# Another order for the prologue and the first row of an adaLN attention/FFN block

## The chip, the cores and the metric

The kernel runs on one core of one Trainium2 chip. The metric is device time in microseconds of one launch; before the change it is 679.94 us (median of 3 runs, 679.27 to 681.49).

## The reference, cut to what matters

```python
mod = (silu(c) @ wmod).reshape(B, 6, 1, D)         # B = 8, D = 256
sa, ca, ga, sb, cb, gb = mod[:, 0..5]              # ga, gb: magnitude at least 0.25
h = layernorm(x) * (1 + ca) + sa                   # x: 8 x 2048 x 256
q, k, v = split(h @ w_qkv + b_qkv)                 # 8 heads of 64
scores = einsum('bhld,bhle->bhde', q, k) / 8       # 64 x 64 per head: over the sequence
attn = softmax(scores)
o = (v @ attn) @ w_fc + b_fc + h
x = x + ga * (layernorm(o) * gamma + beta)
h = layernorm(x) * (1 + cb) + sb
xr, xk = mu * h + (1 - mu) * previous_token(h)     # mu_r, mu_k
x = x + gb * sigmoid(xr @ W_r.T) * (relu(xk @ W_k.T)**2 @ W_v.T)
```

## The kernel before, in words

The scores of a head are 64 x 64 and sum over the sequence. So the kernel first forms, per batch row, the 256 x 256 Gram matrix of the normalised x ("gram"), multiplies it from both sides with the scaled q and k weights (`gram_q`, `scores`), takes the softmax, folds v weights, attention and output weights into one 256 x 256 matrix M (`wv_attn`, the v product, and `make_m`), and then applies M to each chunk (`attention`). All is fp32; the products with M and with W_v are made of three products of high and low parts, `m_hi`, `m_lo`, `z_hi`, `z_lo` (helper `mm3`, L1239 to L1241).

A batch row (b = 0..7) has four chunks j of 512 tokens, and each chunk four tiles of 128 tokens. The rows are software-pipelined: `row_steps(b)` does the second half of row b (attention, residual and second layernorm, FFN) beside the first half of row b + 1 (statistics, normalisation, Gram matrix, softmax, M). The prologue is the first half of row 0, and `row_steps(0, first=True)` has an order of its own; rows 1 to 6 are a hardware loop, and row 7 has `last_row`.

The order on each engine is written out by hand, and engines wait for each other on semaphores with counts. An engine works through its own program in order. Its parts, by engine:

- VectorE (DVE): `stats_a` (L902), `make_z` (L912, the first normalisation), `low_z` (L992), softmax (L1070 to L1087), `take_vb` (L863), `make_m` (L1094 `m_sb`, L1097 `m_hi`, L1099 `m_lo`), `prep_now` (L1039, waits for the row `ca` from DRAM), `make_x2` (L924 and L929), `stats_2` (L935 to L945), `mix_r` and `mix_k` (L957, L966), `prep_qk` (L1047), `low_k` (L1000).
- GpSimd (POOL): `rstd_a` (L460 to L472: nine small operations, the reciprocal root of a chunk's variance), `rstd_o` (L485, L487), `rstd_2` (L478, L480), `bias_wv` (L509, which completes `wv_aug`), `fill_x2` (L492, a DMA from its queue that adds x to the rows waiting in `x2`).
- ScalarE (ACT): `copy_z_hi` (L618), `squares` (L652), `copy_pv` (L642), `copy_weights` (L612), `prep_base_qk` (L709, L710), `make_z2` (L717), `copy_h2` (L661), `scale_r`, `scale_k` (L670, L679), `take_r`, `take_k`.
- TensorE (PE): `turn_and_gram` (transposes L1348, Gram products L1355), `attention` (L1239 to L1241 into `att`), `turn_z2` (L1392), `ffn_r` (L1408), `ffn_k` (L1425), `ffn_out` (L1239 to L1241 into `work`), `turn_ffn` (L1330, transposes of the three FFN weights), `wv_attn` (L1479), `make_m` (L1488), `bias_v` (L1292), `mod_b_columns` (L1263).
- SyncE (SP): loads and stores. `next_ca(1)` loads the row `ca` of row 1 (L312) once M of row 0 is ready.

There are eight PSUM banks: `gram`, `tr0` and `tr1` (all transposes), `att0` and `att1` (attention's output), `work0` to `work2` (FFN). `attention(b, j)` may write `att` only when VectorE has read the chunk before it out of there (`t_done`). `turn_and_gram(b, j)` for j of 2 and 3 waits until ScalarE has taken the transposed `z2` of chunk j - 2 out of `tr` (`h2_ready`).

The first part of TensorE's row 0 was

```python
attention(b, 0)
turn_and_gram(n, 0)
attention(b, 1)
turn_and_gram(n, 1)
turn_z2(b, 0)
attention(b, 2)
turn_and_gram(n, 2)
```

with n = b + 1.

## Time and profile before

| | us |
|---|---|
| median of 3 runs | 679.94 |
| lowest and highest | 679.27, 681.49 |
| the profiled execution, its own time | 681.61 |
| its span, first to last instruction | 679.8 |
| PE busy | 654.6 |
| DVE busy | 567.8 |
| ACT busy | 457.0 |
| POOL busy | 294.0 |

The profile is of one execution. Times in it count from the first instruction. Prologue and row 0 up to the last step that the change moves lie in the first 98 us. The granted TensorE clock is 0.991 on average over the span: 1.00 means 2.4 GHz, 0.50 means 1.2 GHz. Busy times of matmuls are modelled ends, so starts are the safer numbers.

### The profile page before, as it was taken

How to read it: one execution, taken by the hardware profiler on the slowest of the kernel's cores; microseconds unless marked ns; L12 is line 12 of the kernel's file. 1: busy time of each engine (PE TensorE's matmuls, PEld its weight loads, DVE VectorE, ACT ScalarE, POOL GpSimd, SP SyncE). 2: the span in 40 equal slices, each digit the busy share in tenths (PEclk: the TensorE clock that was granted, in tenths of full speed). 3: DMA queues.
4: the chain of work that ended last, by engine and by line, in shares of the span. 5: the costliest groups of instructions: out<-in, count | busy, mean ns of one | idle time of the engine just before them, and what ended most of it. 6: DMA issues, size and time to landing. Idle time of an engine off the chain costs nothing.

```text
span 679.8 us, 12488 instructions
## 1 busy us (share of the span) xinstructions
PE 654.6 (96%) x3968; PEld 535.5 (79%) x3968; DVE 567.8 (84%) x1328; ACT 457.0 (67%) x983; POOL 294.0 (43%) x499
## 2 busy tenths in 40 slices
PE   8978799999999999999999999999999999999896
PEld 6657777889869887889878888798878888697665
DVE  5893988889798897889888897889888897859973
ACT  1423767676966779667867769577776769667662
POOL 5263452764318442574227542383327643215230
PEclk9988999999999999999999999999999999999999
DMA  8859237384854958086765758268673737537325
GB/s 315 224 166 198 89 113 160 61 182 123 195 111 83 230 109 208 31 167 165 162 123 100 170 125 204 79 108 224 129 156 62 128 84 169 101 76 154 63 32 92
DMA packets 90985, 93.04 MB, mean 137 GB/s; under 512 B 4224, under 2 KB 89000, under 8 KB 90960
## 3 DMA queue, kind: packets, MB, share of 16 engines
q0 software_dynamic: 33264, 33.03, 32.9%
q1 hardware_dynamic: 55344, 55.97, 26.1%
q10 hardware_dynamic: 2352, 3.73, 1.5%
q8 instruction: 12, 0.20, 0.1%
...
HBM read 42.84 MB, written 33.10 MB: 112 GB/s over the span
## 4 chain that ended last, share of the span: by engine, by line
PE 85%; DVE 7%; POOL 2%; ACT 2%; DMA 2%; issue 2%; DVEq 0%; POOLq 0%; ACTq 0%
PE work L1408 14%; PE work L1425 14%; PE gram L1355 10%; PE att L1239 4%; PE work L1239 4%; PE gram L1488 4%; PE work L1240 4%; PE work L1241 4%; PE att L1241 4%; PE att L1240 4%; PE tr L1392 4%; PE att L1460 4%; PE tr L1348 3%; PE att L1479 2%; PE gram L1470 1%
## 5 line engine op out<-in xcount | busy, mean ns | idle before, releaser
L478 POOL TENSOR_TENSOR rs<-ve,neg_half 128x4 f32<-128x4 f32 x32 | 37.4, 1170 | 179.3 <-DVE ve L945 179.3
L1425 PE MATMUL work<-mx,w_k_t 128*128 128x512 f32 x244 | 109.9, 592 | 0.0
L1408 PE MATMUL work<-w_r_t,mx 128*128 128x256 f32 x464 | 106.0, 381 | 0.3 <-DVE mx L983 0.3
L717 ACT ACTIVATE z<-x,nm,rs 128x256 f32<-128x256 f32 x128 | 66.4, 594 | 46.5 <-POOL nm L480 46.5
L1408 PEld LDWEIGHTS work<-w_r_t,mx 128*128 128x128 f32 x464 | 85.8, 190 | 11.8 <-DVE mx L983 0.5
L1355 PE MATMUL gram<-z 128*128 128x256 f32 (+1 forms) x512 | 89.1, 327 | 0.0
L1355 PEld LDWEIGHTS gram<-z 128*128 128x128 f32 x512 | 79.8, 191 | 6.6
L1425 PEld LDWEIGHTS work<-mx,w_k_t 128*128 128x128 f32 x244 | 46.3, 190 | 46.0 <-issue 42.4
L1239 PE MATMUL att<-m_lo,z_hi 128*128 128x256 f32 x248 | 74.9, 302 | 3.8 <-issue 2.0
L1239 PE MATMUL work<-wvf_lo,k_hi 128*128 128x256 f32 x248 | 72.0, 290 | 2.5 <-issue 2.5
L1240 PE MATMUL att<-m_hi,z_hi 128*128 128x256 f32 x248 | 70.8, 285 | 0.0
L1241 PE MATMUL att<-m_hi,z_lo 128*128 128x256 f32 x248 | 70.7, 285 | 0.0
L1241 PE MATMUL work<-wvf_hi,k_lo 128*128 128x256 f32 x248 | 69.1, 279 | 0.0
L1240 PE MATMUL work<-wvf_hi,k_hi 128*128 128x256 f32 x248 | 69.1, 278 | 0.0
L652 ACT ACTIVATE sq<-att 128x256 f32<-128x256 f32 x124 | 45.7, 381 | 33.1 <-PE att L1241 33.1
L924 DVE SCALAR_TENSOR_TENSOR t_buf<-att,rs_o,g_row 128x256 f32<-128x256 f32 x124 | 51.4, 477 | 10.7 <-POOL rs_o L487 9.9
L485 POOL TENSOR_TENSOR ve_o<-ssq,eps_att 128x4 f32<-128x4 f32 x32 | 17.0, 531 | 94.0 <-ACT sq L652 94.0
L661 ACT ACTIVATE h2t<-tr,mod_now 128x512 f32<-128x512 f32 x64 | 46.4, 781 | 15.2 <-PE tr L1392 15.2
L1000 DVE TENSOR_TENSOR k_lo<-work,k_hi 128x512 fp32r<-128x512 f32 x60 | 40.6, 689 | 18.7 <-ACT k_hi L702 18.5
L492 POOL DMA_DIRECT2D x<-in_L_attn_x_dram x32 | 55.2, 1823 | 0.0
L957 DVE SCALAR_TENSOR_TENSOR mx<-h2t,rest_col,mx 128x512 f32<-128x512 f32 x56 | 39.4, 745 | 17.5 <-ACT mx L670 17.5
L1239 PEld LDWEIGHTS att<-m_lo,z_hi 128*128 128x128 f32 x248 | 48.0, 193 | 7.5 <-issue 7.5
...
## 6 DMA issues: line engine op xcount, KB each, us to landing
...
```

The source lines that it names most:

```text
L492: nc.gpsimd.dma_start(x2[:, j], x_v[b, j], accum_op=ALU.add).then_inc(x2_filled[j], 16)
L652: ins = nc.scalar.activation(sq[:, t], att_banks(j, alone)[t // 2][:, (t % 2) * D:(t % 2 + 1) * D], ACT.Square, scale=float(D) ** -0.5, ac ...
L661: nc.scalar.activation(h2t[:, h, 1 + j * CT:1 + (j + 1) * CT], tr[h][:], ACT.Identity, bias=mod_now[:, h:h + 1], scale=mod_now[:, 2 + h:3 ...
L717: ins = nc.scalar.activation(z2[:, t], x2[:, j, t], ACT.Identity, bias=nm_2[:, s, t:t + 1], scale=rs_2[:, s, t:t + 1])
L924: ins = nc.vector.scalar_tensor_tensor(t_buf[:, t], att_banks(j, alone)[t // 2][:, (t % 2) * D:(t % 2 + 1) * D], rs_o[:, s, t:t + 1], g_ro ...
L1000: nc.vector.tensor_tensor(lo[:, h], k_banks(alone)[h][:], hi[:, h].bitcast(F32), ALU.subtract).then_inc(k_lo_ready, 1)
L1239: mm(dst, s_hi, m_lo, start=start, stop=False)
L1240: mm(dst, s_hi, m_hi, start=False, stop=False)
L1241: return mm(dst, s_lo, m_hi, start=False, stop=stop)
L1355: ins = mm(gram[:, k * D:(k + 1) * D - k * P], z[:, j % 2, t, k * P:(k + 1) * P], z[:, j % 2, t, k * P:D], start=(j == 0 and t == 0 and k ...
L1408: ins = mm(r_banks(alone)[q][:, (t % 2) * D:(t % 2 + 1) * D], mixed(j)[0][:, ch, tile], w_r_t[:, ch], start=(ch == 0), stop=(ch == KD - 1))
L1425: ins = mm(k_banks(alone)[dh][:], w_k_t[:, ch, rows_dh], mixed(j)[1][:, ch], start=(ch == 0), stop=(ch == KD - 1))
```

## The change

VectorE, prologue: the softmax of row 0 and `take_vb` come before the statistics of row 1; the statistics of chunks 2 and 3 of row 1 move from row 0 into the prologue, before `make_m(0)`; `make_z(1, 1)` goes behind `make_m(0)`. In row 0, `make_z(1, 2)` moves from behind `stats_2(0, 1)` to before `low_z(1, 0)`.

GpSimd: `bias_wv` comes before both `rstd_a` of the prologue; the four `fill_x2` are issued in two pairs between the `rstd_a` calls; `rstd_a(1, 2)` moves into the prologue; `rstd_o(0, 1)` goes before `rstd_2(0, 0)`.

TensorE: `wv_attn(0)` goes before `turn_ffn`. In row 0, chunk 0 of row 1 is transposed and multiplied before the first attention; `attention(0, 1)` writes the banks `work0` and `work1`, which the FFN doesn't use yet, and follows `attention(0, 0)` at once; `attention(0, 2)` goes before `turn_z2(0, 0)`. `turn_and_gram(b, 0)` waits on `m_step` (the Gram bank is read) in place of `m_ready` (M is split).

ScalarE: `copy_pv(0)` before the copies of the FFN weights; `squares(0, 1)` read the spare banks.

```diff
@@ -77,8 +77,9 @@
         def k_banks(alone):
             return (gram, work[2]) if alone else (work[1], work[2])
 
-        def att_banks(j, alone):
-
+        def att_banks(j, alone, spare=False):
+            if spare:
+                return work[0:2]
             return tr if alone and j == 1 else att
 
 
@@ -518,17 +519,16 @@
 
                 n = b + 1
                 rstd_o(b, 0)
-                if not first:
+                if first:
+                    rstd_o(b, 1)
+                else:
                     add_y(b - 1, 2)
                     fill_x2(b, 2)
                 rstd_2(b, 0)
                 if first:
-
-                    rstd_o(b, 1)
-                    rstd_a(n, 2)
+                    rstd_a(n, 3)
                     rstd_2(b, 1)
                     rstd_o(b, 2)
-                    rstd_a(n, 3)
                 else:
                     rstd_o(b, 1)
                     rstd_2(b, 1)
@@ -570,11 +570,14 @@
             for j in range(CH):
                 rstd_a(0, j)
             prep_wv()
+            bias_wv()
             rstd_a(1, 0)
+            fill_x2(0, 0)
+            fill_x2(0, 1)
             rstd_a(1, 1)
-            bias_wv()
-            for j in range(CH):
-                fill_x2(0, j)
+            rstd_a(1, 2)
+            fill_x2(0, 2)
+            fill_x2(0, 3)
             row_steps(0, True, True)
             with pool.Fori(1, B - 2) as b:
                 row_steps(b, False, True)
@@ -642,14 +645,14 @@
                     nc.scalar.activation(pv_t[:, 2 * g:2 * g + 2].rearrange("p n d -> p (n d)"), att[g][:],
                                          ACT.Copy).then_inc(pv_ready, 1)
 
-            def squares(b, j, alone=False):
+            def squares(b, j, alone=False, spare=False):
 
                 i, s = CH * b + j, j % 2
                 wait_past(act, ssq_ready, i)
                 for t in range(NT):
                     if t % 2 == 0:
                         act.wait_ge(att_done, 2 * i + t // 2 + 1)
-                    ins = nc.scalar.activation(sq[:, t], att_banks(j, alone)[t // 2][:, (t % 2) * D:(t % 2 + 1) * D], ACT.Square,
+                    ins = nc.scalar.activation(sq[:, t], att_banks(j, alone, spare)[t // 2][:, (t % 2) * D:(t % 2 + 1) * D], ACT.Square,
                                                scale=float(D) ** -0.5, accum_out=ssq[:, s, t:t + 1])
                 ins.then_inc(ssq_ready, 1)
 
@@ -725,7 +728,7 @@
                 copy_z_hi(n, 0)
                 prep_base_qk(n)
                 if first:
-                    squares(b, 1)
+                    squares(b, 1, spare=True)
                     copy_z_hi(n, 1)
                     make_z2(b, 0)
                 else:
@@ -807,8 +810,8 @@
             copy_gram_low(0)
             copy_gq(0)
             exps(0)
+            copy_pv(0)
             copy_weights(2, [(w_r_t[:], tr[0]), (w_k_t[:], tr[1]), (w_v_t[:], work[0])])
-            copy_pv(0)
             row_steps(0, True)
             with act.Fori(1, B - 1) as b:
                 row_steps(b, False)
@@ -913,7 +916,7 @@
                                                   ag_a[:, j, 7, t:t + 1], ALU.subtract, ALU.mult)
                 ins.then_inc(z_ready, 1)
 
-            def make_x2(b, j, mixes=0, alone=False):
+            def make_x2(b, j, mixes=0, alone=False, spare=False):
 
                 i, s = CH * b + j, j % 2
                 wait_past(dve, x2_ready, i)
@@ -921,8 +924,8 @@
                     dve.wait_ge(xk_mixed, CH * b + mixes)
                 dve.wait_ge(rs_o_ready, i + 1)
                 for t in range(NT):
-                    ins = nc.vector.scalar_tensor_tensor(t_buf[:, t], att_banks(j, alone)[t // 2][:, (t % 2) * D:(t % 2 + 1) * D],
-                                                         rs_o[:, s, t:t + 1], g_row[:], ALU.mult, ALU.mult)
+                    src = att_banks(j, alone, spare)[t // 2][:, (t % 2) * D:(t % 2 + 1) * D]
+                    ins = nc.vector.scalar_tensor_tensor(t_buf[:, t], src, rs_o[:, s, t:t + 1], g_row[:], ALU.mult, ALU.mult)
                 ins.then_inc(t_done, 1)
                 dve.wait_ge(t_done, i + 1)
                 dve.wait_ge(x2_filled[j], 16 * (b + 1))
@@ -1103,16 +1106,15 @@
                 n = b + 1
                 take_g(b)
                 prep_now(n)
+                if first:
+                    make_z(n, 2)
                 low_z(n, 0)
                 make_x2(b, 0)
                 stats_2(b, 0)
                 if first:
-                    stats_a(n, 2)
-                    stats_a(n, 3)
                     low_z(n, 1)
-                    make_x2(b, 1)
+                    make_x2(b, 1, spare=True)
                     stats_2(b, 1)
-                    make_z(n, 2)
                 else:
                     low_k(b - 1, 3)
                     make_z(n, 2)
@@ -1210,15 +1212,17 @@
             low_z(0, 3)
             centre_fc()
             make_rest()
-            stats_a(1, 0)
-            stats_a(1, 1)
             softmax_dif(0)
             take_vb()
             softmax_norm(0)
+            stats_a(1, 0)
+            stats_a(1, 1)
+            take_mod_col(1, mod_b_done, work[2])
+            stats_a(1, 2)
             make_z(1, 0)
+            stats_a(1, 3)
+            make_m(0)
             make_z(1, 1)
-            take_mod_col(1, mod_b_done, work[2])
-            make_m(0)
             dve.wait_ge(mod_col_ready, 2)
             dve.wait_ge(rest_ready, 1)
             dve.wait_ge(w_copied, 5)
@@ -1348,7 +1352,7 @@
                         ins = nc.tensor.transpose(tr[h][:, t * P:(t + 1) * P], z[:, j % 2, t, h * P:(h + 1) * P], ident[:])
                     ins.then_inc(z_turned, 1)
                 if j == 0 and not first:
-                    pe.wait_ge(m_ready, b)
+                    pe.wait_ge(m_step, 2 * b - 1)
                 for t in range(NT):
                     for k in range(KD):
 
@@ -1357,11 +1361,15 @@
                                  skip_group_check=True)
                 ins.then_inc(z_used, 1)
 
-            def attention(b, j, alone=False):
+            def attention(b, j, alone=False, spare=False, after_spare=False):
                 i = CH * b + j
                 pe.wait_ge(m_ready, b + 1)
                 pe.wait_ge(z_lo_ready, 2 * i + 2)
-                if not alone:
+                if after_spare:
+                    pe.wait_ge(t_done, i - 1)
+                elif spare:
+                    pass
+                elif not alone:
                     wait_past(pe, t_done, i)
                 elif j == 1:
                     pe.wait_ge(h2_ready, 2 * CH * b)
@@ -1371,7 +1379,7 @@
                     for t in (2 * q, 2 * q + 1):
                         tile = slice(t * P, (t + 1) * P)
                         for k in range(KD):
-                            ins = mm3(att_banks(j, alone)[q][:, (t % 2) * D:(t % 2 + 1) * D],
+                            ins = mm3(att_banks(j, alone, spare)[q][:, (t % 2) * D:(t % 2 + 1) * D],
                                       (z_hi[:, j, k, tile], z_lo[:, j, k, tile], m_hi[:, k], m_lo[:, k]),
                                       start=(k == 0), stop=(k == KD - 1))
                     ins.then_inc(att_done, 1)
@@ -1491,17 +1499,23 @@
             def row_steps(b, first):
 
                 n = b + 1
-                attention(b, 0)
-                turn_and_gram(n, 0)
-                if not first:
+                if first:
+                    turn_and_gram(n, 0)
+                    attention(b, 0)
+                    attention(b, 1, spare=True)
+                    turn_and_gram(n, 1)
+                    attention(b, 2, after_spare=True)
+                    turn_z2(b, 0)
+                else:
+                    attention(b, 0)
+                    turn_and_gram(n, 0)
                     ffn_r(b - 1, 3)
                     ffn_k(b - 1, 3)
-                attention(b, 1)
-                if not first:
+                    attention(b, 1)
                     ffn_out(b - 1, 3)
-                turn_and_gram(n, 1)
-                turn_z2(b, 0)
-                attention(b, 2)
+                    turn_and_gram(n, 1)
+                    turn_z2(b, 0)
+                    attention(b, 2)
                 turn_and_gram(n, 2)
                 ffn_r(b, 0)
                 ffn_k(b, 0)
@@ -1563,8 +1577,8 @@
             scores(0)
             bias_v()
             mod_b_columns()
+            wv_attn(0)
             turn_ffn()
-            wv_attn(0)
             pe.wait_ge(fc_ready, 1)
             make_m(0)
             pe.wait_ge(w_copied, 5)
```

TensorE from the scores to the first attention, before (`y` holds the FFN weights that are transposed, `gq` and `wfc_c` are the operands of `make_m`):

```order
L1470 MATMUL gram<-wqk_aug,gq 64x64 x16
L1292 MATMUL work<-mod_col,wqkv_sb 128x8 x8
L1263 MATMUL work<-silu,h2t 128x8 x8
L1330 MATMUL tr<-ident,y 128x128 x8
L1330 MATMUL work<-ident,y 128x128 x4
L1479 MATMUL att<-wv_aug,attn 128x256 x4
L1488 MATMUL gram<-wfc_c,gq 128x256 x8
L1239 MATMUL att<-m_lo,z_hi 128x256
L1240 MATMUL att<-m_hi,z_hi 128x256
```

and in the changed kernel:

```order
L1478 MATMUL gram<-wqk_aug,gq 64x64 x16
L1296 MATMUL work<-mod_col,wqkv_sb 128x8 x8
L1267 MATMUL work<-silu,h2t 128x8 x8
L1487 MATMUL att<-wv_aug,attn 128x256 x4
L1334 MATMUL tr<-ident,y 128x128 x8
L1334 MATMUL work<-ident,y 128x128 x4
L1496 MATMUL gram<-wfc_c,gq 128x256 x8
L1352 MATMUL tr<-ident,z 128x128 x8
L1359 MATMUL gram<-z 128x256
```

The v product (`att<-wv_aug,attn`) now stands before the 12 transposes, and the transposes and Gram products of chunk 0 of row 1 (`tr<-ident,z`) before attention.

VectorE from the start of M's last steps to the normalisation of chunk 2, before:

```order
L1094 TENSOR_TENSOR m_sb<-gram,res 128x512
L1097 CAST m_hi<-m_sb 128x512
L1099 TENSOR_TENSOR m_lo<-m_sb,m_hi 128x512
L1018 COPY g_row<-rows 128x256
L1019 COPY mod_now<-mod_col 128x4
L1039 TENSOR_SCALAR neg_d<-rows 128x1
L1040 COPY d_now<-mod_col 128x2
L992 TENSOR_TENSOR z_lo<-tr,z_hi 128x512 x2
L924 SCALAR_TENSOR_TENSOR t_buf<-att,rs_o,g_row 128x256 x4
L929 TENSOR_TENSOR x<-t_buf,x 128x1024
L935 BN_STATS st<-x 128x6 x4
```

and in the changed kernel:

```order
L1102 TENSOR_TENSOR m_lo<-m_sb,m_hi 128x512
L915 TENSOR_SCALAR z<-x_in,ag_a 128x255 x4
L1021 COPY g_row<-rows 128x256
L1022 COPY mod_now<-mod_col 128x4
L1042 TENSOR_SCALAR neg_d<-rows 128x1
L1043 COPY d_now<-mod_col 128x2
L915 TENSOR_SCALAR z<-x_in,ag_a 128x255 x4
L995 TENSOR_TENSOR z_lo<-tr,z_hi 128x512 x2
L928 SCALAR_TENSOR_TENSOR t_buf<-att,rs_o,g_row 128x256 x4
L932 TENSOR_TENSOR x<-t_buf,x 128x1024
L938 BN_STATS st<-x 128x6 x4
```

Two normalisations (`z<-x_in`) have come into this stretch: that of chunk 1 behind `m_lo`, and that of chunk 2 behind the wait for `rows` (the row `ca`).

## Rows read from the trace of the kernel before

**Rows 1.** TensorE's waits, 40 to 150 us, then 93 to 680: total, times, longest.

```profile
PE att L1479 <- POOL wv_aug L509: 2.2, 1, 2.2
PE att L1239 <- issue: 2.0, 1, 2.0
PE tr L1348 <- DVE z L912: 1.5, 1, 1.5
...
PE work L1239 <- issue: 2.5, 3, 0.9
```

**Rows 2.** Timeline, 41 to 48 us: start, us, engine, line, out<-in, count, [idle before].

```profile
41.00 1.15 PE L1470 MATMUL gram<-wqk_aug,gq 128*64 128x64 f32 x32 [0.69 <-ACT gq L633]
43.89 1.93 PE L1263 MATMUL work<-silu,h2t 128*128 128x8 f32 x16
44.76 0.86 DVE L1070 TENSOR_REDUCE s_max<-gram 64x4 f32<-64x256 f32 x2
46.54 0.63 DVE L863 TENSOR_SCALAR vb_col<-work,bv_col 128x8 f32<-128x8 f32 x4
47.08 0.41 DVE L1081 TENSOR_REDUCE s_sum<-s_exp 128x4 f32<-128x256 f32 x1
```

**Rows 3.** Timeline, 45 to 60 us.

```profile
45.68 1.13 PE L1330 MATMUL tr<-ident,y 128*128 128x128 f32 x8
48.65 3.69 DVE L912 TENSOR_SCALAR z<-x_in,ag_a 128x255 f32<-128x255 f32 x8
49.71 5.47 POOL L492 DMA_DIRECT2D x<-in_L_attn_x_dram  x4
49.90 3.69 PE L1479 MATMUL att<-wv_aug,attn 128*128 128x256 f32 x8 [2.24 <-POOL wv_aug L509]
54.36 3.69 PE L1488 MATMUL gram<-wfc_c,gq 128*128 128x256 f32 x16 [0.78 <-ACT gq L642]
59.28 0.69 DVE L1099 TENSOR_TENSOR m_lo<-m_sb,m_hi 128x512 fp32r<-128x512 f32 x1
```

**Rows 4.** Windows: stretch, its length, busy of each engine, granted clock, DMA.

```profile
46.60:46.80 0.20, 0.20 (x3) 0.20 (x2) 0.20 (x2) 0.20 (x1) 0.20 (x3) 0.50 1.03 343
53.40:53.60 0.20, 0.18 (x1) 0.00 (x0) 0.00 (x0) 0.00 (x0) 0.20 (x2) 1.00 1.08 174
60.20:60.40 0.20, 0.20 (x2) 0.20 (x3) 0.06 (x1) 0.00 (x0) 0.00 (x0) 0.54 1.15 184
```

**Rows 5.** Windows: PE, PEld, DVE, ACT, POOL busy, granted clock, DMA.

```profile
67.30:97.70 30.40, 26.02 (x167) 22.22 (x165) 29.88 (x79) 21.09 (x48) 16.79 (x28) 1.00 0.32 104
100.00:134.00 34.00, 34.00 (x197) 26.07 (x196) 28.60 (x64) 26.13 (x54) 13.93 (x29) 1.00 0.49 112
```

**Rows 6.** Timeline of row 0, 64 to 98 us.

```profile
64.29 0.15 DVE L1039 TENSOR_SCALAR neg_d<-rows 128x1 f32<-128x1 f32 x1 [4.04 <-DMA rows<-row_scratch]
72.30 2.70 DVE L902 BATCH_NORM_STATS2 st_a<-x_in 128x6 f32<-128x256 f32 x8
78.22 1.34 ACT L670 ACTIVATE mx<-h2t,mu_col 128x512 f32<-128x512 f32 x2
81.12 1.37 DVE L912 TENSOR_SCALAR z<-x_in,ag_a 128x255 f32<-128x255 f32 x4
96.39 1.28 DVE L1000 TENSOR_TENSOR k_lo<-work,k_hi 128x512 fp32r<-128x512 f32 x2
```

**Rows 7.** GpSimd's timeline: the ends of one `rstd_a` and of another.

```profile
43.61 0.20 POOL L460 TENSOR_TENSOR ag_a<-st_a 128x4 f32<-128x4 f32 x1 [2.40 <-DVE st_a L902]
45.45 1.01 POOL L472 TENSOR_TENSOR ag_a<-ag_a,neg_half 128x4 f32<-128x4 f32 x1
...
86.41 1.19 POOL L460 TENSOR_TENSOR ag_a<-st_a 128x4 f32<-128x4 f32 x1
91.75 1.01 POOL L472 TENSOR_TENSOR ag_a<-ag_a,neg_half 128x4 f32<-128x4 f32 x1
```

**Rows 8.** The page, costliest groups: busy, mean ns of one, idle before.

```profile
L652 ACT ACTIVATE sq<-att 128x256 f32<-128x256 f32 x124 | 45.7, 381 | 33.1 <-PE att L1241 33.1
```

## The prediction, made before the changed kernel was run

> **What bounds the kernel now.** I read the page first. TensorE is busy 654.6 of 679.8 us, 96% of the span, so time can only come out of places where it stands still or runs at the lower of its two clocks. The waits of TensorE say where these are: all waits of over a microsecond lie before 93 us, and from 93 us to the end there are 5.3 us in total, of which the line with the most is 2.5 us in three places [rows 1]. Everything the change moves lies in the prologue and in row 0, before 94 us. From 100 to 134 us TensorE is busy for all 34.00 of 34.00 us [rows 5]: what arrives earlier at 97.7 us therefore arrives earlier at the end, as long as the other engines are earlier by as much.
>
> Then the timeline, where three chains follow each other.
>
> Up to 46 us it is the softmax of row 0. The scores end at 42.15 (41.00 + 1.15), but VectorE starts on the row maxima only at 44.76, behind two chunks of statistics of row 1 [rows 2]. On GpSimd the copy that completes `wv_aug` stands behind the two `rstd_a` calls which those statistics feed, and that copy is what TensorE waits for, 2.2 us, until the v product starts at 49.90 [rows 1, 3].
>
> From 49.9 to 60 us it is the v product, `make_m` on TensorE, then three VectorE steps that end at 59.97 (59.28 + 0.69) [rows 3]. TensorE waits 2.0 us for them [rows 1]. The granted clock falls twice: at about 46.6 us, behind 3.7 us of products of only 8 columns, to come back at 53.4; and at 60.2, behind the wait of 2.0 us [rows 4]. So the eight instructions of the v product take 3.69 us.
>
> From 67.30 to 97.67 us (96.39 + 1.28) it is VectorE alone: busy 29.88 of 30.40 us there [rows 5, 6]. Its program runs from `make_x2(0, 0)` to the end of `low_k(0, 0)`, and `ffn_out(0, 0)` of TensorE waits for that.
>
> **The change, part by part**, on the profiled execution (span 679.8 us, own time 681.61; the median of the three runs, 679.94, is 1.7 lower, and I take the difference over to it).
>
> *Softmax first.* VectorE starts the maxima at 42.2. Maxima, differences and the exponential took from 44.76 to 47.0, when the sums start, so they end at 44.5. `take_vb` (0.63 us) waits for `bias_v` on TensorE, which ends as the next product starts, 43.89 [rows 2]; it is through at 44.7. The sums and the division took 47.08 to 48.65, 1.57 us [rows 2, 3]: 46.3. GpSimd completes `wv_aug` at 45.1, since `bias_wv` is now ahead of both `rstd_a`. TensorE is free at 45.8 and starts the v product at 46.4 instead of 49.90.
>
> *ffn transposes behind it.* They no longer stand before the v product, and on ScalarE `copy_pv` goes ahead of their copies, so `pv_t` is made while TensorE transposes. But the clock falls at about 46.6 [rows 4], as what runs before that is not changed. I therefore keep 3.6 us for the v product: 50.0. The lower bound would be the 1.89 us that it would take with the clock up, half of 3.69, rounded up. The 12 transposes follow at the upper clock: eight are busy for 1.13 us, modelled end included [rows 3], so 1.4 to 1.7 for all: 51.4. `make_m` takes 3.69 (16 instructions against the 8 of the v product in the same time, so its row is at the upper clock): 55.1 instead of 58.05. VectorE needs its 1.9 us from there (58.05 to 59.97): `m_ready` at 57.0, **3.0 us earlier**. The statistics of chunks 0 to 3 of row 1 (four at 1.35, half of the 2.70 for two [rows 6]) and `make_z(1, 0)` lie on VectorE between 46.3 and 54, inside TensorE's 8.7 us; they cost nothing, and if that cover were gone would cost up to 1 us.
>
> *Gram of chunk 0 ahead of attention.* With the wait on `m_step` TensorE needs only the first of the three VectorE steps for `gram`, and the transposes need none. The chunk takes 3.5 us at the upper clock (82.55 to 86.0 in the timeline), so it ends at 58.6, and `attention(0, 0)` and, in the spare banks, `attention(0, 1)` follow to 61.5 and 64.4, at 2.9 each (69.1 to 72.0 in the timeline). So the wait of 2.0 and the second fall of the clock go here.
>
> *What VectorE does until `make_x2(0, 0)`.* The row `ca` is loaded only once `m_ready` is there; before, VectorE waited 4.04 us for it, to 64.29, which is 4.3 us after `m_ready` [rows 3, 6]. With the same 4.3 it comes at 61.3, plus 0.25 for the two small ones. Now `make_z(1, 2)` stands there: 1.37 us alone [rows 6], but eight such took 3.69 beside GpSimd's DMAs [rows 3], 0.46 each, so 1.37 to 1.85. Then `low_z(1, 0)`, 1.3: 64.2 to 64.7. ScalarE's squares of chunk 0 end 0.9 behind attention, 62.4, `z_hi` at 63.5, in time. I take **64.5** against 67.30: 2.8 us.
>
> *GpSimd's queue.* In its program: `rstd_a(1, 0)`, two DMAs, `rstd_a(1, 1)`, `rstd_a(1, 2)`, two DMAs, and only then `rstd_o(0, 0)`. An `rstd_a` undisturbed takes 2.85 us (43.61 to 46.46), four DMAs took 5.47 [rows 3, 7]. From 47.7 on: 3 x 2.85 + 5.5 = 14.0, so 61.8, before the squares at 62.4; `rs_o` at 63.7 is in time. `make_z(1, 1)` needs `rs_a` at 56.3 and has it. The upper bound is an `rstd_a` as at 86.41 to 92.76, 6.35 us, beside VectorE's weight preparation [rows 7]. I take 2.85, since VectorE runs mostly statistics here, as it did at 43.6.
> On that row the Trainium skill, "SBUF — State Buffer", section Who interferes with whom, says that a VectorE instruction with two SBUF inputs holds off a GpSimd instruction that reads SBUF. By it only `m_lo` here would collide, and the sum would stay; it is the ground of the third rival.
>
> *VectorE's long stretch.* Two chunks of statistics (2.70 us) and `make_z(1, 2)` (1.37) leave it [rows 6]: **4.1 us**. What shortens it uncovers waits. T is the start of `make_x2(0, 0)`. Before, `scale_r` ended at 79.56, T + 12.3, by way of the statistics, GpSimd, `make_z2`, the transposes and `copy_h2`. VectorE came to `make_z` at 81.12, T + 13.8; without the 2.70 it is there, and now at `mix_r`, at T + 11.1 [rows 6]: a wait of 1.2, of which I take 1.1, as T + 12.3 is the end of both halves. `low_z(1, 2)` then needs `z_hi` behind ScalarE's `scale_k` (1.3, as `scale_r`), four squares (1.5 [rows 8]) and the copy itself, an estimated 0.6 for the first half, as a square takes 0.38 with half the columns: T + 15.7, against VectorE free at T + 15.0: 0.6 more. Third, TensorE has done `attention(0, 2)` at 71.0 and waits for `z2` until 73.3, 2.3 us. At 2.0 us the clock had fallen [rows 1, 4], at 1.5 us (the wait for z) it had not, so I count on a fall: the eight transposes take 0.9 more, 0.6 of it passes to `copy_h2`. Sum of the waits 2.3.
> After that TensorE has `turn_and_gram(1, 2)`, `ffn_r`, `ffn_k`, two of them at 3.5 us, and reaches `attention(0, 3)` near 88, about when VectorE has freed the banks; `low_k(0, 0)` comes last, as before.
>
> *In the loop* nothing changes: there `attention` waits for a later point than the new wait on `m_step`.
>
> **Sum:** 2.8 + 4.1 − 2.3 = **4.6 us**. 679.94 − 4.6 = **675.3 us**.
>
> **The rivals.**
>
> *More is won* (0.13). The clock holds through the v product and does not fall at 73 either. `m_ready` would be 1.8 earlier, at 55.2, but then GpSimd's queue (61.8 + 1.3) sets T to 63.1. 4.2 + 4.1 − 1.7 = 6.6: 673.3. Against it: the clock row at 46.60 stands before anything that differs.
>
> *The `ca` row lands late* (0.10). It is issued at 57.0, 4 to 6 us behind the first two fills of `x2`, where it used to follow the four at a distance of 5 to 10. If it took 7.0 us instead of 4.3, VectorE would stand from 58.7 to 64, and the gain would be 4.6 − 2.7 = 1.9: 678.0. For it: transfers overlap more. Against: only two fills are in flight, not four. It is also the case in which the order does what it says and little is seen.
>
> *GpSimd comes late* (0.04), the one on the other side. `rstd_o(0, 0)` now stands behind two `rstd_a` and all four fills. If both `rstd_a` took 6.35 us [rows 7] and the fills twice their 5.47, GpSimd would be there at 61.8 + 7.0 + 5.5 = 74.3, T at 75.6, and the sum 67.3 − 75.6 + 4.1 − 1.7 = −5.9: 685.8. It decides from T = 69.7 on (67.3 + 4.1 − 1.7), that is, from GpSimd being 6.6 us later than I compute (68.4 + 1.3 = 69.7). Against it: those 6.35 us lay beside VectorE's instructions with two SBUF inputs, and hardly any stand here.
>
> **How the numbers follow.** The forecast has 0.73; its own bounds (0.5 at `make_z`, 0.6 for the clock, 0.5 at the waits) give 674.0 to 676.8. The range takes in the first rival and the second: 672.8 to 678.2. A difference under 0.3%, 2.0 us, can hardly be told from none here. Faster by more than that: the forecast, the first rival and the nearer half of a late `ca` row, 0.88; within it 0.08; slower 0.04.
>
> **What would show it.** In the profile of the changed kernel: v product from about 46.4 with some 3.6 us, `make_m` to 55, `m_lo` to 57; no wait between `make_m` and the transposes; VectorE waiting for `rows` until 61 and `make_x2(0, 0)` at 64.5; TensorE waiting some 2.3 us for `z2` and about 1 us for `h2t` behind it; `low_k(0, 0)` ending near 93 and no new idle after 100. The prediction is wrong if `rs_o` is what `make_x2(0, 0)` waits for, if the v product takes 1.9 us, or if TensorE finds a wait after 97 us that it did not have.

## The result and the profile after

| | before | after |
|---|---|---|
| median, six runs each, us | 679.61 | 676.57 |
| lowest and highest | 678.53, 681.49 | 675.36, 677.16 |
| the profiled execution, its own time | 681.61 | 675.36 |
| its span | 679.8 | 673.7 |

The ratio is 0.995, 95% interval 0.9935 to 0.9965: 3.0 us less, or 0.4%. A second comparison, on another occasion, gave 677.44 against 680.17, ratio 0.9958 (0.9945 to 0.9971), 2.7 us. The two traces above differ by more, 6.1 us. That difference is taken up below.

The page of the changed kernel, its span and the busy time of the engines:

```profile
span 673.7 us, 12495 instructions
PE 655.3 (97%) x3968; PEld 537.0 (80%) x3968; DVE 568.9 (84%) x1328; ACT 456.6 (68%) x983; POOL 289.5 (43%) x499
```

TensorE, VectorE and ScalarE work as long as before, to 1.1 us, and GpSimd 4.5 us less (289.5 against 294.0), but it is busy for less than half of the span. The span around TensorE's work is shorter. Its waits from 40 to 150 us, in the view of rows 1 (who waited for whom: total, times, longest):

```profile
PE tr L1400 <- ACT z L720: 2.2, 1, 2.2
PE tr L1352 <- ACT h2t L664: 1.2, 1, 1.2
```

The waits for `wv_aug` (2.2), for M (2.0) and for `z` of chunk 2 (1.5) of rows 1 are gone. A wait of 2.2 us for `z2` and one of 1.2 us for `h2t` have come. The timeline of the changed kernel, prologue and row 0, answers to rows 2, 3 and 6 (start, duration, engine, line, out<-in, count, idle before; SPq and POOL DMA rows are issues):

```profile
41.90 0.87 DVE L1073 TENSOR_REDUCE s_max<-gram 64x4 f32<-64x256 f32 x2
...
45.88 3.59 PE L1487 MATMUL att<-wv_aug,attn 128*128 128x256 f32 x8 [0.36 <-DVE attn L1090]
49.26 1.18 PE L1334 MATMUL tr<-ident,y 128*128 128x128 f32 x8
50.13 2.85 POOL L493 DMA_DIRECT2D x<-in_L_attn_x_dram  x2
50.71 3.62 PE L1496 MATMUL gram<-wfc_c,gq 128*128 128x256 f32 x16
...
55.55 0.69 DVE L1102 TENSOR_TENSOR m_lo<-m_sb,m_hi 128x512 fp32r<-128x512 f32 x1
56.27 0.33 SPq L313 DMA_DIRECT2D rows<-row_scratch  x1
59.45 0.15 DVE L1042 TENSOR_SCALAR neg_d<-rows 128x1 f32<-128x1 f32 x1 [1.62 <-DMA rows<-row_scratch]
59.67 2.64 POOL L493 DMA_DIRECT2D x<-in_L_attn_x_dram  x2
59.76 2.17 DVE L915 TENSOR_SCALAR z<-x_in,ag_a 128x255 f32<-128x255 f32 x4
62.26 1.29 DVE L995 TENSOR_TENSOR z_lo<-tr,z_hi 128x512 fp32r<-128x512 f32 x2 [0.33 <-ACT z_hi L621]
62.62 1.03 POOL L488 TENSOR_TENSOR rs_o<-ve_o,neg_half 128x4 f32<-128x4 f32 x1
63.68 1.66 DVE L928 SCALAR_TENSOR_TENSOR t_buf<-att,rs_o,g_row 128x256 f32<-128x256 f32 x4
...
75.86 1.42 DVE L960 SCALAR_TENSOR_TENSOR mx<-h2t,rest_col,mx 128x512 f32<-128x512 f32 x2 [0.86 <-ACT mx L673]
79.01 1.29 DVE L995 TENSOR_TENSOR z_lo<-tr,z_hi 128x512 fp32r<-128x512 f32 x2 [0.41 <-ACT z_hi L621]
90.32 1.28 DVE L1003 TENSOR_TENSOR k_lo<-work,k_hi 128x512 fp32r<-128x512 f32 x2
```

M is ready at 56.24 (55.55 + 0.69) against 59.97. `make_x2(0, 0)`, the row `t_buf<-att`, starts at 63.68 against 67.30. `low_k(0, 0)`, the last row, ends at 91.60 against 97.67. This is 6.07 us earlier, and the span is 6.1 us shorter. So nothing was won or lost behind 98 us. The same holds in all twelve other traces of this study: the span is 581.5 to 582.3 us longer than the time at which `low_k(0, 0)` ends. So the span of every traced execution below can be read from that one row. A trace shows one execution, though, and its own time can lie 2.5 us from the median of its kernel, so that it is given with each.

The granted clock of the changed kernel, windows as in rows 4:

```profile
46.00:46.20 0.20, 0.20 (x1) 0.18 (x2) 0.20 (x2) 0.00 (x0) 0.00 (x0) 0.79 1.06 348
49.20:49.40 0.20, 0.20 (x2) 0.14 (x1) 0.20 (x2) 0.00 (x0) 0.20 (x1) 0.50 0.03 10
49.60:49.80 0.20, 0.20 (x4) 0.20 (x3) 0.20 (x2) 0.20 (x1) 0.20 (x1) 1.00 0.00 0
73.40:73.60 0.20, 0.01 (x1) 0.00 (x0) 0.20 (x2) 0.20 (x1) 0.20 (x1) 0.56 0.00 0
80.00:81.00 1.00, 1.00 (x7) 0.95 (x7) 1.00 (x2) 0.00 (x0) 0.00 (x0) 0.88 0.00 1
```

The granted clock is the last number but two of a row. It falls to its lower level (1.2 GHz) at about 46.1, in the first of the eight v products, and is back (2.4 GHz) at 49.6, so that most of the ffn transposes run at the upper level. It falls once more at 73.4, in the wait for `h2t`, and is back between 80 and 81. The fall of rows 4 at 60.2 is gone.

### The profile page after: what moved, and what is told of

It reads as the page before. It is cut to its first block, busy times and chain, and to the rows that moved or that the text cites. A ratio compares the mean times of both kernels' runs of the same rounds, so it can differ in the third digit from the quotient of the medians.

```text
span 673.7 us, 12495 instructions
## 1 busy us (share of the span) xinstructions
PE 655.3 (97%) x3968; PEld 537.0 (80%) x3968; DVE 568.9 (84%) x1328; ACT 456.6 (68%) x983; POOL 289.5 (43%) x499
## 4 chain that ended last, share of the span: by engine, by line
PE 87%; DVE 4%; POOL 3%; ACT 2%; DMA 2%; issue 1%; DVEq 0%; POOLq 0%; ACTq 0%
PE work L1433 15%; PE work L1416 15%; PE gram L1359 11%; PE work L1243 4%; PE att L1468 4%; PE work L1244 4%; PE work L1245 4%; PE att L1243 4%; PE tr L1400 4%; PE att L1244 4%; PE att L1245 4%; PE tr L1352 4%; PE gram L1496 4%; PE att L1416 2%; PE att L1487 2%; PE gram L1478 1%
## 5 line engine op out<-in xcount | busy, mean ns | idle before, releaser
L1359 PE MATMUL gram<-z 128*128 128x256 f32 (+1 forms) x512 | 91.1, 332 | 0.0
L1359 PEld LDWEIGHTS gram<-z 128*128 128x128 f32 x512 | 81.4, 195 | 7.1
L1243 PE MATMUL att<-m_lo,z_hi 128*128 128x256 f32 x240 | 71.8, 299 | 0.1
L1244 PE MATMUL att<-m_hi,z_hi 128*128 128x256 f32 x240 | 67.8, 282 | 0.0
L1245 PE MATMUL att<-m_hi,z_lo 128*128 128x256 f32 x240 | 67.8, 282 | 0.0
L655 ACT ACTIVATE sq<-att 128x256 f32<-128x256 f32 x120 | 44.1, 380 | 29.7 <-PE att L1245 29.7
L928 DVE SCALAR_TENSOR_TENSOR t_buf<-att,rs_o,g_row 128x256 f32<-128x256 f32 x120 | 49.7, 477 | 10.7 <-POOL rs_o L488 9.8
L692 ACT ACTIVATE y<-work 128x512 f32<-128x512 f32 x58 | 32.4, 585 | 29.6 <-PE work L1416 29.5
```

The costliest lines, as they stand in the source:

```text
L655: ins = nc.scalar.activation(sq[:, t], att_banks(j, alone, spare)[t // 2][:, (t % 2) * D:(t % 2 + 1) * D], ACT.Square, scale=float(D) ** - ...
L928: ins = nc.vector.scalar_tensor_tensor(t_buf[:, t], src, rs_o[:, s, t:t + 1], g_row[:], ALU.mult, ALU.mult)
L1243: mm(dst, s_hi, m_lo, start=start, stop=False)
L1244: mm(dst, s_hi, m_hi, start=False, stop=False)
L1245: return mm(dst, s_lo, m_hi, start=False, stop=stop)
L1359: ins = mm(gram[:, k * D:(k + 1) * D - k * P], z[:, j % 2, t, k * P:(k + 1) * P], z[:, j % 2, t, k * P:D], start=(j == 0 and t == 0 and k ...
```

## Experiments

Each was timed in five rounds beside the kernel before, except the third trace of before. "M ready" is the end of `m_lo`, T the start of `make_x2(0, 0)`. What the row `ca` "took" is the time from its issue by SyncE to the first instruction of VectorE that reads it (`neg_d<-rows`), which waited for it in every trace. The kernels ran on three occasions, on which before had medians of 680.17, 679.85 and 680.27, so that kernels of different occasions are best compared by their ratios.

### The two kernels again

The kernel before and the changed kernel, unchanged, for a second trace of each.

> The kernel before, unchanged, profiled again. The two traces differ by 6.1 us (679.8 and 673.7), the medians of six by 3.0 (679.61 and 676.57). If the profiled execution of before was a long one of its kind (its own time 681.61 lies 2.0 above its median), this trace has a span near 677.8 and shows where the 2 us lie: in the places where the clock falls. If instead the trace is near 679.8, the 6.1 us stand and the difference of the medians is what needs an explanation. Time: 679 to 680, ratio 1.00.

> The changed kernel, unchanged, profiled again. Time 676 to 677, gain 3 to 4 us. Its first trace (own time 675.36) was the shortest of six. If the spread comes from when the clock falls, this trace is up to 1.5 us longer with a lower mean clock than 0.988, and the extra stands between 46 and 50 us, at 73 us or in the last row, not in the loop.

Before: 679.95 us, ratio 0.9994 (0.9984 to 1.0004), the traced execution 681.66, span 679.8. So the trace was again one of the long ones, one of the two longest of twelve, and the first way of reading was not borne out: `low_k(0, 0)` ends at 97.83. The 6.1 us stand, and it is the difference of the medians that needs an explanation. A typical execution was not seen. Changed kernel: 677.44, and the traced execution, 677.48, is a typical one. Its timeline, in the same stretch:

```profile
50.16 1.91 PE L1334 MATMUL tr<-ident,y 128*128 128x128 f32 x8
52.68 3.62 PE L1496 MATMUL gram<-wfc_c,gq 128*128 128x256 f32 x16
57.52 0.71 DVE L1102 TENSOR_TENSOR m_lo<-m_sb,m_hi 128x512 fp32r<-128x512 f32 x1
58.27 0.33 SPq L313 DMA_DIRECT2D rows<-row_scratch  x1
61.25 0.15 DVE L1042 TENSOR_SCALAR neg_d<-rows 128x1 f32<-128x1 f32 x1 [1.45 <-DMA rows<-row_scratch]
64.24 1.29 DVE L995 TENSOR_TENSOR z_lo<-tr,z_hi 128x512 fp32r<-128x512 f32 x2 [1.13 <-ACT z_hi L621]
65.45 1.65 DVE L928 SCALAR_TENSOR_TENSOR t_buf<-att,rs_o,g_row 128x256 f32<-128x256 f32 x4
92.10 1.28 DVE L1003 TENSOR_TENSOR k_lo<-work,k_hi 128x512 fp32r<-128x512 f32 x2
```

The ffn transposes take 2.5 us from 50.16 to `make_m`, where the first trace had 1.45: the clock is still at its lower level (0.84 on average from 52 to 54 us, 1.00 there in the first trace). With a prologue 0.7 us later from the start on (v product at 46.59 against 45.88) this makes M ready at 58.23, 2.0 us later than in the first trace, and the end 1.8 us later. The expectation had named the place (from 46 us on) and put it at up to 1.5 us with a lower mean clock; the mean clock is higher (0.991 against 0.988). From T on the two agree: 27.92 and 27.93 us to the end of `low_k(0, 0)`, where before took 30.37.

### One part alone: the prologue

```diff
@@ POOL, prologue
-            rstd_a(1, 0)
-            rstd_a(1, 1)
             bias_wv()
+            rstd_a(1, 0)
+            rstd_a(1, 1)
@@ ACT, prologue
+            copy_pv(0)
             copy_weights(2, ...)
-            copy_pv(0)
@@ DVE, prologue
-            stats_a(1, 0)
-            stats_a(1, 1)
             softmax_dif(0)
             take_vb()
             softmax_norm(0)
+            stats_a(1, 0)
+            stats_a(1, 1)
@@ PE, prologue
-            turn_ffn()
             wv_attn(0)
+            turn_ffn()
```

> Only the prologue part: softmax and take_vb before the statistics of row 1, bias_wv before both rstd_a, v product before the ffn transposes, copy_pv first; row 0 as before. Theory (the prediction's first term, 3.0 us, is a shift of M that row 0 passes on in full): M ready 3 to 3.7 us earlier, make_x2(0, 0) at 63.6 to 64.3 in place of 67.3, total gain 3.0 to 3.5, with the wait of 2.0 us before attention and its fall of the clock still there. Rival (VectorE's stretch and not M sets the end, so an earlier M is only waited away): gain under 1 us.

682.50 us, ratio 1.0037 (1.0024 to 1.005): slower, by 2.3 us. Neither theory said so. The timeline of this kernel:

```profile
53.74 5.47 POOL L492 DMA_DIRECT2D x<-in_L_attn_x_dram  x4
57.69 0.69 DVE L1099 TENSOR_TENSOR m_lo<-m_sb,m_hi 128x512 fp32r<-128x512 f32 x1
58.41 0.33 SPq L312 DMA_DIRECT2D rows<-row_scratch  x1
65.68 0.15 DVE L1039 TENSOR_SCALAR neg_d<-rows 128x1 f32<-128x1 f32 x1 [6.78 <-DMA rows<-row_scratch]
67.01 1.65 DVE L924 SCALAR_TENSOR_TENSOR t_buf<-att,rs_o,g_row 128x256 f32<-128x256 f32 x4
```

M is ready 1.6 us earlier than in before, not the 3 to 3.7 expected. And the row `ca`, issued at 58.41, is there only at 65.68, after 7.3 us, where before it took 4.3. Four fills of `x2`, 512 KB each, were issued from 53.74 to 59.2, ahead of it and around it. VectorE waits 6.78 us and starts `make_x2(0, 0)` at 67.01. This is the prediction's second rival, stronger than it was priced. In the trace it takes the gain away: T is 0.3 us earlier than in the trace of before, and `low_k(0, 0)` ends 0.15 us earlier. The loss of 2.3 us stands in the medians alone. The traced execution (681.51) is the shortest of five here, 1.0 below its median, and that of before (681.61) is above its own, so no trace shows where the 2.3 us are lost.

### One part alone: row 0

```diff
@@ from the changed kernel: PE, ACT, DVE and POOL prologue in the order of before, with
+            stats_a(1, 2)
+            stats_a(1, 3)
             make_m(0)
@@ DVE, and on POOL
             bias_wv()
+            fill_x2(0, 0)
+            fill_x2(0, 1)
+            rstd_a(1, 2)
+            fill_x2(0, 2)
+            fill_x2(0, 3)
```

> Only the row-0 part, with the statistics of chunks 2 and 3 of row 1 in the prologue behind make_z(1, 1); prologue otherwise as before. Theory: M ready at 60.0 as before, the ca row at 64.3, make_z(1, 2) and low_z behind it, so make_x2(0, 0) at 67.3 to 68.0; VectorE's stretch 4.1 us shorter less 2.3 of new waits; gain 1.2 to 1.8. The two parts then add up to 4.6 to 5. Rival (the prologue part is what makes the row part pay): no gain or a loss.

680.17 us, ratio 1.0003 (0.9995 to 1.0012): no difference. The traced execution has 679.82. T is 67.91, within what was expected, but by luck: M is ready 1.2 us before the 60.0 expected (58.09 + 0.69), and the row `ca` comes 1.0 us later than expected (65.27 for 64.3). VectorE's stretch is as short as in the changed kernel (27.92 us). The issue of the row and its landing:

```profile
56.16 2.67 POOL L493 DMA_DIRECT2D x<-in_L_attn_x_dram  x2
58.81 0.33 SPq L313 DMA_DIRECT2D rows<-row_scratch  x1
65.27 0.15 DVE L1042 TENSOR_SCALAR neg_d<-rows 128x1 f32<-128x1 f32 x1 [6.21 <-DMA rows<-row_scratch]
```

Here too the row takes long, 6.5 us, with two fills just ahead of it. The two parts alone give +2.3 and 0.0 us, together −2.7 to −3.0. They are not two terms of a sum, because what lies between them, the row `ca`, depends on both. In the traces row 0 alone does gain, 1.7 us of span (678.1 against 679.8), and in the medians nothing: the same gap between the traced and the typical execution of before as above.

### The prologue with the fills apart

```diff
@@ from the prologue-only kernel, POOL
             rstd_a(1, 0)
+            fill_x2(0, 0)
+            fill_x2(0, 1)
             rstd_a(1, 1)
-            for j in range(CH):
-                fill_x2(0, j)
@@ row_steps, first
                 rstd_o(b, 0)
+                fill_x2(b, 2)
+                fill_x2(b, 3)
@@ DVE: make_z(1, 1) behind make_m(0)
```

> The prologue-only kernel again, with the fills of x2 placed as in the change: two behind rstd_a(1, 0), the other two behind rstd_o(0, 0), and make_z(1, 1) behind make_m(0). In the prologue-only kernel the ca row was issued at 58.4 just behind four fills (53.7 to 59.2) and took 7.3 us; in the changed kernel it took 3.2 us. Theory (the ca row, held up by the fills in flight, ate the 3 us of the earlier M): the row lands within 4.5 us of its issue, make_x2(0, 0) starts at 64.0 to 65.0, the time is 3 us below that of the prologue-only kernel (682.5), 678.5 to 679.8. Rival (an earlier M is waited away in any case): 681.5 to 682.5 with the row early.

679.64 us, ratio 0.9996 (0.9984 to 1.0008), so 2.9 us below the prologue-only kernel. The theory's range for it was 678.5 to 679.8. Two things differ from the prologue-only kernel, the fills and the place of `make_z(1, 1)`. From the start of `make_m` to M ready it takes 0.6 us less (50.05 to 55.58 against 52.27 to 58.38), which can come from the place of `make_z(1, 1)`; the row `ca` takes 4.1 us less, with two fills ahead of it and not four. Its timeline:

```profile
49.50 2.85 POOL L492 DMA_DIRECT2D x<-in_L_attn_x_dram  x2
55.62 0.33 SPq L312 DMA_DIRECT2D rows<-row_scratch  x1
58.81 0.15 DVE L1042 TENSOR_SCALAR neg_d<-rows 128x1 f32<-128x1 f32 x1 [1.66 <-DMA rows<-row_scratch]
61.68 1.29 DVE L995 TENSOR_TENSOR z_lo<-tr,z_hi 128x512 fp32r<-128x512 f32 x2 [2.64 <-ACT z_hi L621]
62.88 1.65 DVE L927 SCALAR_TENSOR_TENSOR t_buf<-att,rs_o,g_row 128x256 f32<-128x256 f32 x4
```

The row takes 3.2 us. Now VectorE waits for `z_hi`, 2.64 us, which is where the changed kernel has put `make_z(1, 2)`. The executions of this kernel lie far apart, 676.9 to 681.2, and the traced one, 677.14, is near the lower end. In it M is ready 4.4 us earlier than in the trace of before, and T follows 7.30 us behind M, with the clock at its lower level from 56 to 59 us (0.51 on average from 56 to 58). Yet the median is that of before. So the earlier M with the fills apart is not enough for a gain in the median, and why it gains nothing at all stays open, since the typical execution of this kernel, 2.5 us longer, was not traced.

### The changed kernel with the fills together

```diff
             rstd_a(1, 0)
-            fill_x2(0, 0)
-            fill_x2(0, 1)
+            for j in range(CH):
+                fill_x2(0, j)
             rstd_a(1, 1)
             rstd_a(1, 2)
-            fill_x2(0, 2)
-            fill_x2(0, 3)
```

> The changed kernel with all four fills behind rstd_a(1, 0), none between rstd_a(1, 2) and rstd_o(0, 0). Theory: the ca row is issued at about 56.3 right behind four fills and takes 6 to 7.5 us instead of 3.2, so VectorE starts make_z(1, 2) at 62.5 to 63.5 instead of 59.8, make_x2(0, 0) at 66 and the time is 1.5 to 3 us above the changed kernel, 678.5 to 680. GpSimd comes 2.7 us later to rstd_a(1, 1) and (1, 2), which the same wait covers. Rival (only GpSimd's queue matters, and it is free earlier for rstd_o): the same time as the changed kernel or up to 0.8 us less.

680.19 us, ratio 0.9994 (0.9983 to 1.0005). This one move takes away all that the change had won. The traced execution, 680.23, is a typical one. Its timeline:

```profile
50.54 5.47 POOL L493 DMA_DIRECT2D x<-in_L_attn_x_dram  x4
58.01 0.33 SPq L313 DMA_DIRECT2D rows<-row_scratch  x1
65.23 0.15 DVE L1040 TENSOR_SCALAR neg_d<-rows 128x1 f32<-128x1 f32 x1 [4.06 <-DMA rows<-row_scratch]
67.86 1.65 DVE L926 SCALAR_TENSOR_TENSOR t_buf<-att,rs_o,g_row 128x256 f32<-128x256 f32 x4
```

7.2 us for the row. It had gone out 2.0 us behind the last of the fills (50.54 + 5.47), and VectorE was waiting for it, not for GpSimd. T is 67.86, 1.9 us later than the 66 expected, because I had put the issue at 56.3 as in the first trace of the changed kernel. Against the second trace of the changed kernel, also a typical execution with M ready at about the same time (57.98 and 58.23), T is 2.4 us later and VectorE's stretch 0.6 longer (28.56), 3.0 us together for 2.7 us between the medians. Two of the twelve executions, 677.67 and 677.77, are as short as the changed kernel; no trace shows what they do.

### The clock held by idle transposes

```diff
@@ in before, PE
+            warm_in(att[0], 17)
             row_steps(0, True)
@@ in the changed kernel, PE, row_steps, first
                     attention(b, 2, after_spare=True)
+                    warm_in(work[2], 19)
                     turn_z2(b, 0)
```

`warm_in` transposes the identity as often as it is told.

> The kernel before, with 17 idle transposes of the identity (into att0, which nobody needs then) in the wait of 2.0 us between make_m(0) and attention(0, 0). In both traces of before the granted clock falls at 60.2 behind that wait and costs attention(0, 0) about 1.5 us. Theory A (it does so in every execution): 1.2 to 1.5 us less, 678.4 to 678.8, smaller spread. Theory B (it falls only in the longer executions, 681 to 682, and the two traces are of those): the median moves by less than 0.7, and the executions above 681 vanish.

> The changed kernel with 19 idle transposes (into work2) between attention(0, 2) and turn_z2(0, 0), where TensorE waits 2.0 to 2.2 us for z2. Theory (the prediction's 0.6 us for the clock, passed on through copy_h2): clock 1.00 from 70 to 82, h2t and low_k(0, 0) 0.3 to 0.8 us earlier, 676.0 to 676.9. In its first trace copy_h2 ran its two halves at 73.0 to 74.5 without a delay, since the clock fell only at 73.3; then the gain is only what TensorE's Gram and ffn_r hand on, 0 to 0.3. Rival (TensorE is late there): over 1 us.

In before: 680.61 us, ratio 1.0008 (0.9992 to 1.0024), the traced execution 680.41 with a span of 677.6. The clock does hold, 1.00 in every window from 54 us on, and T comes 5.80 us behind M instead of 7.33:

```profile
58.71 0.69 DVE L1099 TENSOR_TENSOR m_lo<-m_sb,m_hi 128x512 fp32r<-128x512 f32 x1
65.20 1.65 DVE L924 SCALAR_TENSOR_TENSOR t_buf<-att,rs_o,g_row 128x256 f32<-128x256 f32 x4
```

So the fall at 60 costs 1.5 us where it happens. Yet the median is no lower, in the own times or in the spans. The median of the spans is 677.95, and that of the kernel before beside it 678.0; the own times are longer than the spans by 1.8 to 4.1 us instead of 1.7 to 1.9, which the trace doesn't explain. This speaks for theory B, that the fall at 60 is not in the typical execution of before, and does not show it: the second thing that B said, that the executions above 681 vanish, did not come (five of twelve are above, two of them, with spans of 680.1 and 681.2, not only by the time outside the span).

In the changed kernel: 677.16, ratio 0.9959 (0.9946 to 0.9973), the traced execution 677.22, against 677.44 for the changed kernel: within what the runs tell apart. The clock is 1.00 from 70 to 84 us, and T to the end of `low_k(0, 0)` is 27.93, as without. The fall that the first trace had at 73.4 costs nothing there: VectorE's waits for `scale_r` and `z_hi` are 0.87 and 0.42 with the clock held, 0.86 and 0.41 without.

### A third trace of before

> The kernel before, unchanged, one more trace. The two that there are belong to executions of 681.6 us, 1.8 above the median of all (679.8). In both the clock falls at 60.2, and make_x2(0, 0) starts 7.3 us behind the end of m_lo; with the clock held there it was 5.8. If this execution has about 679.8 us, its distance is 5.8, that is, the clock does not fall at 60, and low_k(0, 0) ends near 96.1. If it is again 681.6, nothing is decided.

One execution, 681.06 us, span 679.3, again above the typical, with the clock falling at 60:

```profile
59.41 0.69 DVE L1099 TENSOR_TENSOR m_lo<-m_sb,m_hi 128x512 fp32r<-128x512 f32 x1
67.42 1.65 DVE L924 SCALAR_TENSOR_TENSOR t_buf<-att,rs_o,g_row 128x256 f32<-128x256 f32 x4
```

7.32 us apart, as in the other two. It decides nothing, as written beforehand. Of the 86 timed executions of before with a span on record, 16 have one of 679.3 us or more, and all three traces are that long (679.8, 679.8, 679.3). That tracing itself lengthens this kernel is not excluded, though the traced executions of the other kernels lie on both sides of their medians.

### No spare banks

```diff
@@ att_banks, attention, squares, make_x2: spare not used
-                if after_spare:
-                    pe.wait_ge(t_done, i - 1)
-                elif spare:
-                    pass
-                elif not alone:
+                if not alone:
                     wait_past(pe, t_done, i)
```

> The changed kernel with attention(0, 1) in the att banks, so that it waits until make_x2(0, 0) has read them (t_done); order unchanged. Theory: attention(0, 1) starts at 67 instead of 62 (2.0 us after make_x2(0, 0) starts), squares(0, 1), turn_and_gram(1, 1) and through it low_z(1, 1) come 3 to 4 us later than VectorE needs them, and the clock may fall in the wait: 2 to 4 us lost, 679.5 to 681. Rival (VectorE hides it): within 1 us of the changed kernel.

682.67 us, ratio 1.0031 (1.0017 to 1.0045): 5 us above the changed kernel, more than the 2 to 4 expected. The traced execution, 682.68, is typical. Its waits of TensorE, and VectorE in the timeline:

```profile
PE att L1243 <- DVE t_buf L928: 6.4, 3, 4.4
```

```profile
73.52 1.29 DVE L995 TENSOR_TENSOR z_lo<-tr,z_hi 128x512 fp32r<-128x512 f32 x2 [3.31 <-ACT z_hi L621]
```

TensorE waits 4.4 us for the banks, runs at 0.50 from 66 to 70 us, and VectorE then waits 3.31 us for chunk 1. `scale_r` comes late too, another 3.13 us of VectorE's waiting. T is early (65.11); the loss is all behind it. In this order, with the Gram products ahead of attention, the spare banks are not an extra but a condition.

### Fills later, and Gram products later

```diff
@@ both: POOL, prologue
             rstd_a(1, 2)
-            fill_x2(0, 2)
-            fill_x2(0, 3)
@@ both: row_steps, first
                 rstd_o(b, 0)
+                    fill_x2(0, 2)
+                    fill_x2(0, 3)
                     rstd_o(b, 1)
@@ the second only: PE, row_steps, first
-                    turn_and_gram(n, 0)
-                    attention(b, 0)
+                    turn_and_gram(n, 0, between=lambda: attention(b, 0))
```

`between` is called behind the transposes and ahead of the Gram products.

> The changed kernel with the fills of chunks 2 and 3 behind rstd_o(0, 0) instead of ahead of it. VectorE's make_z(1, 2) took 1.7 to 2.2 us beside them and GpSimd's first step of rstd_o 0.7; both go back to 1.4 and 0.2. Theory: in the traces make_x2(0, 0) waits for z_hi (0.3 to 1.1 us), so that this hides what is won: 0 to 0.4 us less than the changed kernel. Rival (GpSimd sets T): 0.5 to 1.0 less.

> As e11, and TensorE transposes chunk 0 of row 1 before attention(0, 0) but forms its Gram products behind it. Attention then starts when M is ready instead of 1.6 us later, and with it the squares and z_hi, which VectorE waited for by 0.3 to 1.1 us. Theory: make_x2(0, 0) 0.8 to 1.3 us earlier than in the changed kernel, 675.6 to 676.4, the best of all. Rival (a wait of 0.9 us behind the transposes makes the clock fall, or the ca row binds): no gain over e11.

With the fills later: 676.66, ratio 0.9946 (0.9934 to 0.9957), the lowest median of its batch. Against the changed kernel's 0.9958 (0.9945 to 0.9971) it is no difference that these runs can tell, and so the theory (0 to 0.4 less) and the rival (0.5 to 1.0 less) are not told apart. In the trace (an execution of 677.38, the longest of six) `make_z(1, 2)` does take 1.38 us again, and the wait for `z_hi` behind it is 1.32. The row `ca`:

```profile
58.60 0.33 SPq L313 DMA_DIRECT2D rows<-row_scratch  x1
61.72 0.16 DVE L1042 TENSOR_SCALAR neg_d<-rows 128x1 f32<-128x1 f32 x1 [1.58 <-DMA rows<-row_scratch]
```

With the Gram products later too: 678.56, ratio 0.9983 (0.9972 to 0.9995), 1.9 us above that. The third way, which I had not thought of:

```profile
62.09 2.22 DVE L915 TENSOR_SCALAR z<-x_in,ag_a 128x255 f32<-128x255 f32 x4 [2.26 <-PE gram L1361]
```

`z` has two buffers. `make_z(1, 2)` overwrites chunk 0, so it waits until the Gram products of chunk 0 have read it (`z_used`). With them behind attention it starts at 62.09 instead of 59.76. The traced execution, 676.80, is the shortest of its twelve, with M ready at 56.17. So the loss does not show in where the trace ends but in the distance from M to T: 9.26 us, against 7.20 with the fills late alone and 7.44 and 7.22 in the two traces of the changed kernel. These 2 us fit the 1.9 us between the medians.

## Why the prediction was right, and where not

Forecast 675.3, range 672.8 to 678.2, faster by more than 0.3%. Measured 676.57: faster, in the range, 3.0 of the 4.6 us. That the two are as near as this is in part luck: the row `ca` came 1.1 us sooner after its issue than was put down, and the step from the trace to the median took too much over.

**M earlier, 3.0 us.** 3.7 and 1.7 us in the two traces (56.24 and 58.23 against 59.97). The v product at the lower clock was right (3.59, 3.78 us for 3.6). What I had as fixed, the transposes behind it at the upper clock, is so in one trace and not in the other: 1.45 and 2.5 us. The prologue up to the scores was taken as it was, too; the scores start at 40.70 and 41.41, against 41.00.

**The `ca` row, 4.3 us as before.** Wrong for a reason that matters. It took 3.2 us (56.27 to 59.45) and 3.0 in the second trace. The row's time goes with the fills ahead of it. In before the row was issued at

```profile
60.00 0.33 SPq L312 DMA_DIRECT2D rows<-row_scratch  x1
```

and all kernels together, the last two columns being the own time of the traced execution, to which T belongs, and the median:

| kernel | fills before the issue | row took, us | T | traced | median |
|---|---|---|---|---|---|
| before | four, 49.7 to 55.2, issue at 60.0 | 4.3 | 67.30 | 681.61 | 679.61 |
| prologue only | four, 53.7 to 59.2, issue at 58.4 | 7.3 | 67.01 | 681.51 | 682.50 |
| prologue, fills apart | two, 49.5 to 52.4, issue at 55.6 | 3.2 | 62.88 | 677.14 | 679.64 |
| row 0 only | two at 49.3, two at 56.2, issue at 58.8 | 6.5 | 67.91 | 679.82 | 680.17 |
| changed, fills together | four, 50.5 to 56.0, issue at 58.0 | 7.2 | 67.86 | 680.23 | 680.19 |
| changed | two, 50.1 to 53.0, issue at 56.3 | 3.2 | 63.68 | 675.36 | 676.57 |
| changed, second trace | two, 50.9 to 53.7, issue at 58.3 | 3.0 | 65.45 | 677.48 | 677.44 |
| changed, fills later | two, 51.3 to 54.2, issue at 58.6 | 3.1 | 65.77 | 677.38 | 676.66 |

That moving the fills moves the row's time is shown by the runs. How the fills hold the row up is not: no row here shows which transfer its data stood behind.

I had this as the second rival, at 0.10, and argued against it that only two fills are in flight. That held, but I costed it at nothing on the gain side. The pairing of the fills, which I took for a matter of GpSimd's queue, is what lets the earlier M through: with the fills together T is 2.4 us later and the gain is gone. How much sooner than 4.3 us the row is matters less: in the second trace VectorE waits 1.13 us for `z_hi` afterwards, so a row 1.1 us later would have left T where it is.

**`make_z(1, 2)` beside GpSimd's DMAs, 1.37 to 1.85.** 2.17 and 1.72 us. T came to 63.68 and 65.45, on both sides of the predicted 64.5.

**VectorE's stretch, 4.1 less 2.3.** From T to the end of `low_k(0, 0)` 27.92 instead of 30.37: 2.45 shorter, for the 1.8 that I had. The two new waits are there and near their size: 0.86 for `scale_r` (1.1), 0.41 for `z_hi` (0.6). The third, 0.6 for the clock, is not. TensorE did wait 2.2 us for `z2` (2.3 predicted) and the clock did fall, but only at 73.4 in the first trace, when the transposes for `copy_h2` were done, and between 76 and 80 in the second, and with the clock held the stretch was just as long.

**The rivals.** The clock did not hold through the v product. GpSimd was late by a hair in the first trace. `rs_o` is there at 63.65 (62.62 + 1.03) and `make_x2(0, 0)` starts at 63.68, 1.42 us behind the start of `low_z(1, 0)`, where it follows by 1.21 in the second trace and in before. So `rs_o` was the last thing it waited for, by 0.2 us, which the prediction had named as a sign of being wrong. Two of the three `rstd_a` ahead of it took 3.9 us each, not 2.85, beside `make_z` and, the first of them, just behind GpSimd's own DMAs, and the fills ended at 62.3 where GpSimd was to be free at 61.8. In the second trace `rs_o` was there 0.3 us ahead of T. The loss of the third rival, 5.9 us, did not come. Of the other signs none was seen: no v product of 1.9 us, and no wait of TensorE behind 97 us that before did not have.

**Two readings that were wrong and decide nothing.** Not all waits of TensorE of over a microsecond lie before 93 us: behind it there is one of 1.3 us for `z2`, in both kernels. And half of 3.69 is 1.85, not 1.89.

**The step that failed** is none of these; together they give 3.6 + 2.45 = 6.1 and 1.85 + 2.45 = 4.3 us in the two traces, 5.2 on average for the predicted 4.6. It is the sentence that the median is 1.7 lower than the traced execution "and I take the difference over to it". The traced executions of before, three by now, took 681.61, 681.66 and 681.06, and the medians were 679.6 to 680.3. The difference of 1.7 us between trace and median was carried over as if the change left it alone. Between the traced execution of before and the one typical trace of the changed kernel (677.48) lie 4.1 us, between the medians 2.7 to 3.0. So the long executions of before hold losses that the typical one does not have, and what the change removed from the trace was in part not there to be removed from the median. The candidate is the fall of the clock at 60.2, 1.5 us where it happens, which the change removes: the span of the first trace less 1.5 is 678.3, and the median span of the 86 timed executions is 678.25. No trace of a typical execution of before was got, so this stays open.
